# Shared-key attention in a two-layer transformer kernel: two batches as one stream of sixteen units

## The chip, the cores and the metric

The kernel runs on one NeuronCore of a Trainium2 chip. The metric is the device time of one execution in microseconds (us); lower is better. One core has TensorE (PE in the profile, with PEld for its weight loads), VectorE (DVE), ScalarE (ACT), GpSimd (POOL), SyncE (SP) and 16 DMA engines. The engines run their own instruction streams and wait for each other on semaphores.

## What is computed

Two transformer layers run on a residual stream of 2 batches x 2048 tokens x 128 channels. Each layer is an attention followed by a mixture-of-experts feed-forward. The change is in the second of the four parts, the attention inside the first layer's feed-forward block. It has four query heads of 32 channels, but one key and one value of 32 channels that all heads share, and it has no mask. Cut to what matters:

```
nx = rmsnorm(X, g1)
Q = (nx @ Wq.T).reshape(B, S, 4, 32).transpose(0, 2, 1, 3)
Kc = nx @ Wkc.T
Vc = nx @ Wvc.T
scores = jnp.einsum('bhsd,btd->bhst', Q, Kc) * scale
attn = jax.nn.softmax(scores, axis=-1)
out = jnp.einsum('bhst,btd->bhsd', attn, Vc)
```

X is layer-normalized first: the statistics of X are folded into the scale of the rmsnorm (rows `S.mean` and `S.rr` of the code).

## The kernel before

The part is `mqa_attention` (L766). Its work is cut into sixteen **units** of 256 queries x 4 heads; units 0 to 7 belong to the first batch, 8 to 15 to the second. Each unit goes through the 2048 keys of its batch in 16 **tiles** of 128 keys. What happens for a unit U:

- `project`: 12 matmuls make its queries (three products each, of parts split into a high and a low float32r half), and ACT (`q_high`) and DVE (`q_low`) copy them into the buffer `qs`.
- `first_pass`: 32 matmuls of 128 queries x 512 keys, each followed by one max over the 512 keys on DVE (`maxima`, L919). They run through three PSUM banks and only serve to find the maximum of every query; `top`, `max_rows` and `max_row` turn it round into the row that is subtracted. They belong to unit U but run during units U-2 and U-1.
- `scores` (L1182): for each tile two matmuls of 128 keys x 512, into one of two halves of the bank group `stb`; ACT takes the exponential of the tile (L1054, 128x1024) into the ring `pt`.
- `values` (L1193): four matmuls per tile, packed in four column groups, add the values up in `pvb`.
- The softmax's denominators: POOL adds the tiles of `pt` in groups of four, 4, 4, 4 and 2 tiles of a unit (L1095 the first add of a group, L1101 the others: ten adds a unit), and PE sums a group over its keys with `sums` (L1201, four matmuls); the last two tiles go through `last_sums` (L1208) without POOL.
- `close`, `evacuate` (ACT, L1037), `post` (PE L1223, DVE L944 and L946): the result is copied out, turned and divided. This happens at the head of the next unit.

PE's order is written out by hand. It is in order, and so is every other engine. In the main loop a unit is eight pairs of tiles, `gi` 0 to 7: scores of the pair, some first passes, values of the pair before, more first passes. The tables say how many first passes stand in a pair. `EARLY` puts 10 first passes of unit U+2 into pairs 5 to 7 of unit U, after unit U+2 was projected at pair 5 (`TURN`). `LATE` puts the other 22 of unit U+1 into pairs 0 to 4. `ALL` puts all 32 of unit U+1 into pairs 0 to 4, where there were no early ones. In this text pairs 0 to 4 up to ACT's `q_high` are a unit's **head** and the rest is its **tail**; a unit is measured from one `evacuate` to the next.

All of this is done once for each batch. `load(b)` makes the batch's keys and values: DVE normalizes four blocks of 512 tokens (L869), PE turns them (L1112), ACT and DVE split them (L1006, L875), PE projects them (L64 to L66 with `wkv`), the keys go to `ks` (L1017, L886), the values are turned once more (L1121) and go to `v1` (L891). Then the first unit of the batch is projected and its 32 first passes run with nothing beside them but their maxima. `ks` and `v1` exist once, so the second batch can't be loaded before the first has ended. Units 7 and 15 have no first passes to do, units 6 and 14 no early ones. POOL also does small jobs at the start of some units (`between`), and DVE at the end of some: statistics, the splitting of later weights, and in units 11 to 15 the normalized copy `x2` (L968).

Of the kernel before, what the change touches and what calls it, by code (L numbers as in the profile page):

```python
# [759 lines left out]
QUADS_OF_TILES = 3  # L760
ADDS = 3 * QUADS_OF_TILES + 1
SUMS_PER_UNIT = QUADS_OF_TILES + 1
# [3 lines left out]
def mqa_attention(nc, dr, X, g, S, wq, wkv, ao, later, x2):  # L766

    m = Mem(nc, "b1_")
    with m:
# [22 lines left out]
        zeroed = m.sem("zeroed")  # L792
        xn_ready = m.sem("xn_ready")
# [56 lines left out]
        def passes_at(u, g, half):  # L850

            if g >= TURN:
                return (u + 2, EARLY[g][half]) if u + 2 < UNITS else (None, 0)
            if u + 1 >= UNITS:
                return None, 0
            return u + 1, (ALL if u == 0 else LATE)[g][half]

        with nc.Block() as block:
            @block.vector
            def _(dve):  # L860
                def norm(b, i):
# [10 lines left out]
                def x_low(b, i):  # L872
                    dve.wait_ge(xh_ready, b * BB + i + 1)
                    cols = slice(i * BLK, (i + 1) * BLK)
                    nc.vector.tensor_tensor(xl[:, cols], stb[:, i, :], xh[:, cols].bitcast(F32),  # L875
                                            ALU.subtract).then_inc(xl_ready, 1)

                def kv_read(b, i):
# [73 lines left out]
                def between(b, u):  # L952
                    if b == 0 and u in (1, 2):
                        stats_vector(nc, dve, X, S, 1e-6, None, (u + 1,))
                    if b == 0 and u == 3:
                        later.scale(nc, dve, (0, 1, 2))
                    if b == 0 and u == 4:
                        later.scale(nc, dve, (3, 4))
                    if b == 0 and u == 5:
                        later.low(nc, dve, (0, 1))  # L960
                    if b == 0 and u == 6:
# [9 lines left out]
                for b in range(BATCH):  # L971
                    load(b)
                    V = b * UNITS
                    dve.wait_ge(zeroed, 3)
                    q_low(V)
                    maxima(V, 0, P1)
                    top(V)
                    max_row(V)
                    q_low(V + 1)
                    for u in range(UNITS):  # L980
                        U = b * UNITS + u
                        if u > 0:
                            begun = planned(EARLY)
                            if u + 1 < UNITS:
                                maxima(U + 1, begun, begun + LATE[0][0])
                            post(U - 1)
                            begun += LATE[0][0]
                        else:
                            begun = 0
                        if u + 1 < UNITS:  # L990
                            maxima(U + 1, begun, P1)
                            top(U + 1)
                        if u + 2 < UNITS:
                            q_low(U + 2)
                        if u + 1 < UNITS:
                            max_row(U + 1)
# [2484 lines left out]
```

## Time and profile before

| | us |
|---|---|
| median of three runs (2077.88 to 2085.22) | 2085.11 |
| the profiled execution, its own time | 2073.83 |
| its span | 2072.0 |
| first exponential of unit 0 | at 597.63 |
| last evacuation of the first batch (unit 7) | at 841.23 |
| first exponential of unit 8 | at 891.23 |
| last evacuation of the second batch (unit 15) | at 1134.73 |
| PE busy / DVE / ACT / POOL over the span | 1747.5 / 1468.5 / 973.3 / 1032.7 |
| mean granted TensorE clock over the span | 0.924 of full |

Times "at" are from the start of the span of the profiled execution. A busy time is the union of an engine's instructions; a PE matmul's duration includes its pipeline, so that consecutive ones overlap and the distance from start to start is what one costs in a stream. A granted clock of 1.00 is 2.4 GHz, 0.50 is 1.2 GHz; a value between them in a stretch is a mean of the two. Rows in order of time give the start in us, how long it lasted in us, engine, line, operation, output and input, how often it stands there, and in brackets the idle time before it and what ended that. Rows of groups by line give, behind the shapes and the count, the busy us, the mean ns of one, and the idle time before them. "Idle before" is the time in which the engine had nothing to do before an instruction, with what it waited for.

### The profile page before, as it was taken

To read this page: it belongs to the slowest core of one execution; us is meant where nothing else is said; L and a number is where in the kernel's file an instruction comes from. 1 tells how busy PE (TensorE), PEld (TensorE's weight loads), DVE (VectorE), ACT (ScalarE), POOL (GpSimd) and SP (SyncE) were. 2 spreads that over 40 slices of the span, in tenths; PEclk is the share of its full clock that TensorE was granted. 3 is DMA by queue.
4 is the path that set the end of the run, shared out by engine and by line. 5 is a ranking of instruction groups with operands and counts; after the bars stand their busy time and mean duration, and the time that the engine had idled before them with its cause. 6 is when DMAs were issued, how large, how long until landed. Compare 5 with 4: busy or idle time off the path is not lost. (4 is left out here: it accounts for less than half of the span.)

```text
span 2072.0 us, 36812 instructions
## 1 busy us (share of the span) xinstructions
PE 1747.5 (84%) x13548; PEld 1314.7 (63%) x13548; DVE 1468.5 (71%) x3418; ACT 973.3 (47%) x2147; POOL 1032.7 (50%) x685
## 2 busy tenths in 40 slices
PE   3799999998599998799997689947899589978993
PEld 2677787776456664456664567635788467757782
DVE  5688777886588884588884678877777777864234
ACT  2455555565226666246565254423333254325664
POOL 3456555655137898258777156653000310265644
PEclk9899999999679999699999789978999889989997
DMA  5112211221100000000000033329500000016763
GB/s 171 70 70 81 76 66 71 78 80 45 42 1 1 2 1 1 0 1 1 2 1 1 1 103 98 99 79 230 111 1 1 1 1 1 15 51 203 206 219 113
DMA packets 78467, 124.07 MB, mean 60 GB/s; under 512 B 11824, under 2 KB 43440, under 8 KB 77776
## 3 DMA queue, kind: packets, MB, share of 16 engines
q1 hardware_dynamic: 73744, 112.31, 17.9%
q0 software_dynamic: 4544, 9.41, 1.3%
q8 instruction: 108, 1.77, 0.4%
q14 instruction: 71, 0.58, 0.1%
HBM read 59.19 MB, written 28.94 MB: 43 GB/s over the span
## 5 line engine op out<-in xcount | busy, mean ns | idle before, releaser
L1054 ACT ACTIVATE mb_pt<-mb_stb 128x1024 f32<-128x1024 f32 x256 | 249.2, 1020 | 136.5 <-PE mb_stb L1182 127.5
L919 DVE TENSOR_REDUCE mb_mxp<-mb_p1b 128x1 f32<-128x512 f32 x352 | 231.1, 683 | 39.5 <-PE mb_p1b L1166 35.5
L1101 POOL TENSOR_TENSOR mb_psum<-mb_psum,mb_pt 128x1024 f32<-128x1024 f32 x96 | 229.2, 2387 | 19.6 <-ACT mb_pt L1054 7.0
L1095 POOL TENSOR_TENSOR mb_psum<-mb_pt 128x1024 f32<-128x1024 f32 x64 | 152.3, 2380 | 164.0 <-ACT mb_pt L1054 164.0
L351 DVE TENSOR_TENSOR ma_tr<-ma_pbank,ma_cs 128x512 f32<-128x512 f32 x256 | 161.7, 682 | 66.3 <-PE ma_pbank L66 53.6
L2478 PE MATMUL mc_pv<-mc_pt,mc_v 128*128 128x256 f32 x544 | 147.0, 395 | 17.6 <-DVE mc_pt L2281 17.4
L441 POOL TENSOR_TENSOR ma_qt<-ma_tr,ma_swp 128x512 f32<-128x512 f32 x64 | 82.1, 1287 | 158.4 <-DMA ma_swp<-ma_tr 147.4
L1166 PE MATMUL mb_p1b<-mb_ks,mb_qs 96*128 96x512 f32 x352 | 152.7, 479 | 6.6 <-DVE mb_qs L912 3.4
L1182 PE MATMUL mb_stb<-mb_qs,mb_ks 98*128 98x512 f32 x512 | 147.5, 409 | 0.8 <-ACT mb_pt L1054 0.8
L1768 POOL TENSOR_TENSOR mc_frs<-mc_fve,mc_half 128x4 f32<-128x4 f32 x8 | 8.1, 1012 | 272.9 <-DVE mc_fve L1752 272.9
L490 ACT ACTIVATE ma_e<-ma_sbank,ma_mx 128x80 f32<-128x80 f32 x512 | 119.1, 365 | 49.8 <-DVE ma_mx L358 49.8
L1605 POOL TENSOR_TENSOR mb_hh<-mb_hh,mb_gb 128x512 f32<-128x512 f32 x64 | 99.2, 1554 | 83.8 <-DVE mb_hh L1622 55.4
L1193 PE MATMUL mb_pvb<-mb_pt,mb_v 128*32 128x256 f32 x2048 | 138.7, 389 | 0.0
L2281 DVE COPY mc_pt<-mc_tb 128x512 f32<-128x512 f32 (+1 forms) x144 | 94.0, 658 | 60.6 <-PE mc_tb L2463 60.2
L919 DVE TENSOR_REDUCE mb_mxp<-mb_misc 128x1 f32<-128x512 f32 x160 | 109.2, 682 | 15.9 <-PE mb_misc L1166 15.9
L1182 PEld LDWEIGHTS mb_stb<-mb_qs,mb_ks 98*128 98x128 f32 x512 | 95.6, 194 | 36.8 <-issue 9.9
L2478 PEld LDWEIGHTS mc_pv<-mc_pt,mc_v 128*128 128x128 f32 x544 | 95.8, 194 | 35.8 <-DVE mc_pt L2281 26.8
L1166 PEld LDWEIGHTS mb_p1b<-mb_ks,mb_qs 96*128 96x128 f32 x352 | 68.0, 200 | 67.5 <-DVE mb_mxp L919 47.6
L443 POOL TENSOR_TENSOR ma_kt<-ma_tr,ma_swp 128x512 f32<-128x512 f32 x64 | 96.4, 1508 | 27.6 <-DMA ma_swp<-ma_tr 24.7
L3121 POOL DMA_INDIRECT d_ret<-md_ys,md_home x78 | 76.8, 984 | 54.8 <-DVE md_ys L3254 37.8
L500 ACT ACTIVATE ma_pt<-ma_fbank 128x512 f32<-128x512 f32 (+1 forms) x160 | 93.2, 583 | 17.0 <-PE ma_fbank L607 17.0
L64 PE MATMUL ma_pbank<-ma_xth,ma_wh 128*128 128x256 f32 x256 | 84.9, 331 | 15.2 <-DVE ma_tr L351 15.2
(405 smaller groups left out, 4759.2 us busy)
## 6 DMA issues: line engine op xcount, KB each, us to landing
ma_swp<-ma_tr SPq DMA_DIRECT2D x256, 128.0 KB, 2.0
md_wslot<-d_weights SPq DMA_DIRECT2D x39, 516.0 KB, 4.0
d_xs<-mw_blank SPq DMA_DIRECT2D x1, 16899.0 KB, 77.1
mb_gb<-b_gates SPq DMA_DIRECT2D x64, 256.0 KB, 3.3
md_xs<-d_xs SPq DMA_DIRECT2D x39, 131.0 KB, 3.3
md_work<-d_ret SPq DMA_DIRECT2D x8, 512.0 KB, 5.8
mg_X<-x SPq DMA_DIRECT2D x4, 512.0 KB, 9.9
ma_cs<-cs SPq DMA_DIRECT2D x1, 2048.0 KB, 9.8
```

What stands on the lines that cost most here:

```text
L351: nc.vector.tensor_tensor(tr[:, G % TRS, part, :, :], pbank[:, i % 2, :].rearrange("p (c t) -> p c t", c=2), cs[:, b // 2, part, None, :]. ...
L443: nc.gpsimd.tensor_tensor(kt[:, par(b), 2 * c:2 * c + 2, :, PM:KEYS0], t0.rearrange("p c (a b) -> p c a b", b=SEG), t1.rearrange("p c (a b ...
L490: nc.scalar.activation(e[:, s, slot, :], sbank[:, 2 * j + k // 4, k % 4 * KEYS0:(k % 4 + 1) * KEYS0], ACT.Exp, bias=mx[:, s, slot:slot + 1 ...
L919: nc.vector.tensor_reduce(mxp[:, r // NCH, r % NCH:r % NCH + 1], pass_bank(r), AXX, ALU.max).then_inc(p1_max, 1)
L1054: nc.scalar.activation(pt[:, T % RING, :, :].rearrange("p (b h) q -> p b (h q)", b=2), stb[:, 2 * (i % 2):2 * (i % 2) + 2, :], ACT.Exp, sc ...
L1095: nc.gpsimd.tensor_tensor(total, pt[:, T % RING, :, :], pt[:, (T + 1) % RING, :, :], ALU.add).then_inc(summed, 1)
L1101: nc.gpsimd.tensor_tensor(total, total, pt[:, (T + i) % RING, :, :], ALU.add).then_inc(summed, 1)
L1166: nc.tensor.matmul(pass_bank(r), qs[V % 3][0:QROWS, h, t * P:(t + 1) * P], ks[0:QROWS, c * BLK:(c + 1) * BLK], start=True, stop=True).then ...
L1182: last = nc.tensor.matmul(stb[:, 2 * (i % 2) + hp, :], ks[:, i * P:(i + 1) * P], qs[U % 3][:, 2 * hp:2 * hp + 2, :].rearrange("p h q -> p ...
L1193: last = nc.tensor.matmul(pvb[h * DK:(h + 1) * DK, 0:UQ], v1[:, i, :], pt[:, T % RING, h, :], start=(i == 0), stop=(i == KT - 1), skip_gro ...
L1605: nc.gpsimd.tensor_tensor(hh[:, t % HR, :], hh[:, t % HR, :], gb[:, q % GBR, :], ALU.mult).then_inc(gated, 1)
L2478: last = nc.tensor.matmul(pv[:, 0:HC * P], v[:, t, :], pt[:, K % 2, a * HC * P:(a + 1) * HC * P], start=(t == 0), stop=(t == r))
```

## The change

`ks` and `v1` now exist twice, once for each batch, and the main loop runs through sixteen units without a break. `load(0)` stays ahead of it. The second batch's blocks 0 and 1 are loaded inside unit 4 and its blocks 2 and 3 inside unit 5 (`LOADS`), in these steps: ACT normalizes the blocks, after each of tiles 1 to 8, with a bias `nbias` that DVE makes once in unit 3; PE turns both blocks after the values of pair 5, into the banks of `p1b`; ACT copies them before tile 12; PE projects keys and values around the values of pair 6, into `misc` and `p1b`; ACT copies the keys after tiles 13 and 14; PE turns the values in pair 7. DVE's parts stand behind `max_row` in a row. So units 4 and 5 have no early first passes, and units 5 and 6 take `ALL` for the unit after them. Units 6 to 13 have early ones, where units 6 and 7 had none. DVE's two later-weight jobs of units 5 and 6 (`later.low`) move to units 6 and 7. In the last two units POOL adds only pairs of tiles (`TWINS`: seven adds a unit for ten), and PE does seven `sums` for four. GpSimd clears the constant rows of two key buffers instead of one before anything starts, and PE's first instruction waits for both (`zeroed` 4).

```
-QUADS_OF_TILES = 3
-ADDS = 3 * QUADS_OF_TILES + 1
-SUMS_PER_UNIT = QUADS_OF_TILES + 1
+FOURS = [(0, 4), (4, 8), (8, 12), (12, 14)]
+TWINS = [(i, i + 2) for i in range(0, KT - 2, 2)]
+SHORT = 2
+LOADS = {4: (0, 1), 5: (2, 3)}
+SUMMED = [TWINS if U >= 2 * UNITS - SHORT else FOURS for U in range(2 * UNITS)]
...
+        ks = [m.sb(f"ks{b}", [QROWS + 2, SEQ], F32R) for b in range(BATCH)]
+        nbias = m.sb("nbias", [P, BT])
+        v1 = [m.sb(f"v1{b}", [P, KT, DK]) for b in range(BATCH)]
...
+            if g >= TURN:
+                return (u + 2, EARLY[g][half]) if early(u) else (None, 0)
+            if u + 1 >= BATCH * UNITS:
+                return None, 0
+            return u + 1, (LATE if early(u - 1) else ALL)[g][half]
+        def early(u):
+            return 0 <= u and u + 2 < BATCH * UNITS and u not in LOADS
...
             @block.vector
...
+                    if early(U):
+                        maxima(U + 2, 0, planned(EARLY))
+                    for i in LOADS.get(U, ()):
+                        x_low(1, i)
+                    for i in LOADS.get(U, ()):
+                        kv_read(1, i)
+                    for i in LOADS.get(U, ()):
+                        v_read(1, i)
...
             @block.scalar
...
+                        if U in LOADS and 1 <= i <= 2 * BPT:
+                            norm(LOADS[U][(i - 1) // BPT], (i - 1) % BPT)
+                        if i == 2 * TURN and U + 2 < BATCH * UNITS:
+                            q_high(U + 2)
+                        if i == 2 * TURN + 1 and U + 1 < BATCH * UNITS:
+                            max_row(U + 1)
+                        if U in LOADS and i == 2 * TURN + 1:
+                            for k in LOADS[U]:
+                                x_high(1, k)
+                        if U in LOADS and i >= 2 * TURN + 3 and i < 2 * TURN + 5:
+                            k_high(1, LOADS[U][i - 2 * TURN - 3])
...
+                    nc.scalar.activation(xn[:, i % 2, s, :], X[:, BT + tile, :], ACT.Identity, bias=nbias[:, tile:tile + 1],
+                                         scale=S.rr[:, BT + tile:BT + tile + 1]).then_inc(xn_ready, 1)
...
             @block.gpsimd
...
-                nc.gpsimd.memset(ks[QROWS:QROWS + 2, :].bitcast(F32), 1.0).then_inc(zeroed, 1)
-                pool.wait_ge(zeroed, 3)
+                for b in range(BATCH):
+                    nc.gpsimd.memset(ks[b][QROWS:QROWS + 2, :].bitcast(F32), 1.0).then_inc(zeroed, 1)
+                pool.wait_ge(zeroed, 4)
...
             @block.tensor
...
-                for b in range(BATCH):
-                    load(b)
...
+                load(0)
+                project(0)
+                for r in range(P1):
+                    first_pass(0, r)
+                max_rows(0)
+                project(1)
+                for U in range(LAST):
...
+                        if U in LOADS and gi == TURN + 1:
+                            pe.wait_ge(m_row0, 2 * U + 4)
+                            pe.wait_ge(m_row1, 2 * U + 4)
+                            keys_values(1, LOADS[U][0])
+                        if U in LOADS and gi == TURN + 2:
+                            turn_values(1, LOADS[U][0])
...
+                        if U in LOADS and gi == TURN:
+                            pe.wait_ge(q_lo, 2 * U + 6)
+                            for i in LOADS[U]:
+                                turn_in(1, i)
+                        if U in LOADS and gi == TURN + 1:
+                            keys_values(1, LOADS[U][1])
+                        if U in LOADS and gi == TURN + 2:
+                            pe.wait_ge(k_lo, BB + LOADS[U][0] + 1)
+                            turn_values(1, LOADS[U][1])
```

How it moves instructions shows at three places. The first is TensorE's tail of unit 4, from behind the sums of pair 5 into pair 7. L1166 (now L1217) are first passes, L1182 (L1233) scores, L1193 (L1246) values, L1201 (L1254) sums. Before:

```order
L1166 MATMUL mb_p1b<-mb_ks,mb_qs 128x512 x2
L1182 MATMUL mb_stb<-mb_qs,mb_ks 128x512 x4
L1166 MATMUL mb_misc<-mb_ks,mb_qs 128x512
L1166 MATMUL mb_p1b<-mb_ks,mb_qs 128x512
L1193 MATMUL mb_pvb<-mb_pt,mb_v 32x256 x8
L1166 MATMUL mb_p1b<-mb_ks,mb_qs 128x512
L1166 MATMUL mb_misc<-mb_ks,mb_qs 128x512
L1182 MATMUL mb_stb<-mb_qs,mb_ks 128x512 x4
L1166 MATMUL mb_p1b<-mb_ks,mb_qs 128x512 x2
L1193 MATMUL mb_pvb<-mb_pt,mb_v 32x256 x8
L1201 MATMUL mb_pvb<-mb_psum,mb_ones 32x256 x4
L1166 MATMUL mb_misc<-mb_ks,mb_qs 128x512
```

And now:

```order
L1155 MATMUL mb_p1b<-mg_ident,mb_xn 128x128 x8
L1233 MATMUL mb_stb<-mb_qs,mb_ks 128x512 x4
L64 MATMUL mb_misc<-mb_xh,mb_wkv 128x512
L65 MATMUL mb_misc<-mb_xh,mb_wkv 128x512
L66 MATMUL mb_misc<-mb_xl,mb_wkv 128x512
L1246 MATMUL mb_pvb<-mb_pt,mb_v 32x256 x8
L64 MATMUL mb_p1b<-mb_xh,mb_wkv 128x512
L65 MATMUL mb_p1b<-mb_xh,mb_wkv 128x512
L66 MATMUL mb_p1b<-mb_xl,mb_wkv 128x512
L1233 MATMUL mb_stb<-mb_qs,mb_ks 128x512 x4
L1171 MATMUL mb_p1b<-mg_ident,mb_vt 128x32 x4
L1246 MATMUL mb_pvb<-mb_pt,mb_v 32x256 x8
```

The ten first passes of unit 6 are gone (nine of them stand above), and eight turns (L1155), six projections (L64 to L66) and eight turns of values (L1171, the second four behind the next sums) stand in their place.

The second is TensorE at the end of unit 7 and the start of the second batch, before the change; behind these rows stood the other blocks, a projection and 32 first passes alone:

```order
L1201 MATMUL mb_pvb<-mb_psum,mb_ones 32x256 x4
L1193 MATMUL mb_pvb<-mb_pt,mb_v 32x256 x8
L1201 MATMUL mb_pvb<-mb_psum,mb_ones 32x256 x4
L1208 MATMUL mb_pvb<-mb_pt,mb_ones 32x256 x8
L1223 MATMUL mb_pvb<-mg_ident,mb_ots 128x128 x4
L1112 MATMUL mb_stb<-mg_ident,mb_xn 128x128 x12
L64 MATMUL mb_p1b<-mb_xh,mb_wkv 128x512
L65 MATMUL mb_p1b<-mb_xh,mb_wkv 128x512
L66 MATMUL mb_p1b<-mb_xl,mb_wkv 128x512
L1112 MATMUL mb_stb<-mg_ident,mb_xn 128x128 x4
```

In the change these rows are gone from this place: behind the close of unit 7 come the first passes of unit 9 and the scores of unit 8, as in every unit.

The third is GpSimd's last two units. Before, in unit 15, adds in groups of three and a single one at the end:

```order
L1101 TENSOR_TENSOR mb_psum<-mb_psum,mb_pt 128x1024 x2
L1095 TENSOR_TENSOR mb_psum<-mb_pt 128x1024
L1101 TENSOR_TENSOR mb_psum<-mb_psum,mb_pt 128x1024 x2
L1095 TENSOR_TENSOR mb_psum<-mb_pt 128x1024
L1101 TENSOR_TENSOR mb_psum<-mb_psum,mb_pt 128x1024 x2
L1095 TENSOR_TENSOR mb_psum<-mb_pt 128x1024
```

And now, the last rows of the part:

```order
L1138 TENSOR_TENSOR mb_psum<-mb_pt 128x1024
L1143 TENSOR_TENSOR mb_psum<-mb_psum,mb_pt 128x1024 x2
L1138 TENSOR_TENSOR mb_psum<-mb_pt 128x1024
L1143 TENSOR_TENSOR mb_psum<-mb_psum,mb_pt 128x1024 x2
L1138 TENSOR_TENSOR mb_psum<-mb_pt 128x1024 x15
```

The row x15 is the single add of unit 13's last group and the fourteen pair adds of units 14 and 15.

## Rows read from the trace of the kernel before

**Rows 1.** Busy time by stretch (us from the span's start): units, loads, heads
```profile
core 0: us, PE busy (x) PEld busy (x) DVE busy (x) ACT busy (x) POOL busy (x), PEclk, DMA share, GB/s
783.43:812.56 29.13, 26.34 (x237) 14.93 (x238) 16.85 (x30) 17.43 (x20) 25.50 (x11) 1.00 0.00 1
812.56:841.23 28.67, 23.91 (x212) 11.40 (x212) 0.63 (x2) 16.59 (x19) 23.54 (x10) 0.88 0.00 1
841.23:866.00 24.77, 16.07 (x60) 10.64 (x60) 14.95 (x36) 6.53 (x11) 0.00 (x0) 0.60 0.00 1
866.00:891.23 25.23, 23.02 (x49) 12.94 (x50) 21.80 (x39) 1.94 (x5) 0.00 (x0) 0.51 0.00 0
891.23:926.42 35.19, 33.09 (x263) 19.04 (x262) 29.50 (x50) 17.44 (x20) 23.76 (x10) 1.00 0.01 2
926.42:956.53 30.11, 29.77 (x259) 18.32 (x260) 24.23 (x42) 18.05 (x21) 23.75 (x10) 1.00 0.01 1
891.23:914.55 23.32, 21.22 (x134) 12.12 (x133) 20.90 (x36) 10.71 (x11) 17.50 (x8) 1.00 0.00 1
926.42:944.67 18.25, 17.91 (x130) 11.43 (x131) 14.87 (x27) 11.31 (x12) 15.03 (x7) 1.00 0.00 0
1077.03:1105.94 28.91, 26.34 (x237) 14.92 (x238) 24.44 (x38) 16.87 (x19) 23.77 (x10) 1.00 0.00 1
1105.94:1134.73 28.79, 23.94 (x212) 11.42 (x212) 8.68 (x9) 16.02 (x17) 23.66 (x10) 0.88 0.01 2
```

**Rows 2.** ScalarE in order of time: last evacuation, next batch's first exponential
```profile
841.23 0.60 ACT L1037 ACTIVATE mb_ots<-mb_pvb 128x512 f32<-128x512 f32 x1 [3.14 <-PE mb_pvb L1208]
...
891.23 1.94 ACT L1054 ACTIVATE mb_pt<-mb_stb 128x1024 f32<-128x1024 f32 x2
```

**Rows 3.** Groups by line, 540 to 1136 us: GpSimd's adds
```profile
L1101 POOL TENSOR_TENSOR mb_psum<-mb_psum,mb_pt 128x1024 f32<-128x1024 f32 x96 | 229.2, 2387 | 19.6 <-ACT mb_pt L1054 7.0
```

**Rows 4.** All engines in order of time, unit 15
```profile
1110.99 1.94 ACT L1054 ACTIVATE mb_pt<-mb_stb 128x1024 f32<-128x1024 f32 x2 [0.63 <-PE mb_stb L1182]
...
1123.51 1.08 PE L1201 MATMUL mb_pvb<-mb_psum,mb_ones 128*32 128x256 f32 x8 [2.27 <-POOL mb_psum L1101]
...
1125.78 1.94 ACT L1054 ACTIVATE mb_pt<-mb_stb 128x1024 f32<-128x1024 f32 x2 [4.20 <-POOL mb_psum L1095]
...
1129.65 1.94 ACT L1054 ACTIVATE mb_pt<-mb_stb 128x1024 f32<-128x1024 f32 x2 [1.93 <-PE mb_stb L1182]
```

**Rows 5.** TensorE in order of time, unit 10, at the full clock
```profile
957.89 0.60 PE L1223 MATMUL mb_pvb<-mg_ident,mb_ots 128*128 128x128 f32 x4
...
977.60 1.09 PE L1182 MATMUL mb_stb<-mb_qs,mb_ks 98*128 98x512 f32 x4
978.53 0.40 PE L1166 MATMUL mb_misc<-mb_ks,mb_qs 96*128 96x512 f32 x1
...
982.13 1.07 PE L1193 MATMUL mb_pvb<-mb_pt,mb_v 128*32 128x256 f32 x16
...
983.57 0.50 PE L1166 MATMUL mb_misc<-mb_ks,mb_qs 96*128 96x512 f32 x1
```

**Rows 6.** Groups by line, 540 to 1136 us: ScalarE's copies; busy us, mean ns
```profile
L1006 ACT ACTIVATE mb_xh<-mb_stb 128x512 fp32r<-128x512 f32 x8 | 4.8, 597 | 16.1 <-PE mb_stb L1112 16.1
L1949 ACT ACTIVATE mb_wkv<-mb_rkv 128x128 fp32r<-128x128 f32 x1 | 0.3, 292 | 0.0
```

**Rows 7.** VectorE in order of time: units 8, 9 and 10
```profile
892.51 1.29 DVE L919 TENSOR_REDUCE mb_mxp<-mb_p1b 128x1 f32<-128x512 f32 x2 [0.59 <-PE mb_p1b L1166]
...
929.19 0.42 DVE L946 TENSOR_TENSOR mb_ao<-mb_pvb,mb_rd 128x256 f32<-128x256 f32 x1
...
957.86 0.69 DVE L919 TENSOR_REDUCE mb_mxp<-mb_p1b 128x1 f32<-128x512 f32 x1 [1.81 <-PE mb_p1b L1166]
```

**Rows 8.** All engines in order of time, start of the part
```profile
547.99 1.80 POOL L1074 MEMSET mb_ks<- 2x2048 f32 x1
...
549.84 1.97 PE L1112 MATMUL mb_stb<-mg_ident,mb_xn 128*128 128x128 f32 x8 [13.43 <-POOL mb_ks L1074]
```

More of the change, by code:

```diff
@@ L969, in between @@
                                                     ALU.subtract, ALU.mult).then_inc(normed, 1)
-                for b in range(BATCH):
-                    load(b)
[L973 to L996, printed above, removed]
-                        if u + 2 < UNITS:
-                            maxima(U + 2, 0, planned(EARLY))
-                        between(b, u)
-                    post(U)
@@ new lines, in _, with passes @@
+                load(0)
+                project(0)
[3 more added lines that the diff above has]
+                project(1)
+                LAST = BATCH * UNITS
+                done = [0] * LAST
+                for U in range(LAST):
+                    def passes(g, half):
+                        w, count = passes_at(U, g, half)
+                        for _ in range(count):
+                            first_pass(w, done[w])
+                            done[w] += 1
+                    for gi in range(PAIRS_OF_TILES):
+                        if gi == 0 and U > 0:
+                            close(U - 1)
+                        scores(U, 2 * gi)
+                        scores(U, 2 * gi + 1)
+                        if gi == TURN and U + 2 < LAST:
+                            project(U + 2)
+                        if gi == TURN and U + 1 < LAST:
+                            max_rows(U + 1)
+                        if U in LOADS and gi == TURN + 1:
[4 more added lines that the diff above has]
+                            turn_values(1, LOADS[U][0])
+                        passes(gi, 0)
+                        if gi == 0 and U > 0:
+                            post(U - 1)
+                        if gi > 0:
+                            values(U, 2 * gi - 2)
+                            values(U, 2 * gi - 1)
+                        for j, (_, end) in enumerate(SUMMED[U]):
+                            if end // 2 + 1 == gi:
+                                sums(U, j)
+                        if U in LOADS and gi == TURN:
[7 more added lines that the diff above has]
+                            turn_values(1, LOADS[U][1])
+                        passes(gi, 1)
```

238 lines of the change are left out of this document (123 added, 115 removed).

## The prediction

> **What bounds the kernel now.** I read three views in this order: busy time by stretch, each engine in order of time, and groups by line. The busy times show three kinds of stretch [rows 1]. In a unit of the steady stream, such as 926.42 to 956.53, PE is busy 29.8 of 30.11 us at clock 1.00 (units 1 to 5 and 9 to 13 are alike), so PE is the bound. Between the last evacuation of the first batch, 841.23, and the first exponential of the second, 891.23 [rows 2], lie 50.0 us in which ACT works 8.5 us and POOL not at all, at a clock of 0.60 and then 0.51: first the load, a chain handed from engine to engine, then 32 first passes that wait for DVE's maxima. And in units 7 and 15 PE has little to do (23.9 us busy), yet they take 28.67 and 28.79 us: POOL is busy 23.5 to 23.7 of it with ten adds of 2.39 us [rows 3], PE's sums wait 2.27 us for one, and an exponential waits 4.20 us for POOL to leave a slot of the ring [rows 4].
>
> One more price is to be read there. A head with all 32 first passes takes 23.32 us in unit 8, one with 22 takes 18.25 us [rows 1]: 0.51 us for each first pass more, although PE spends only 0.23 us on one (four 512-column matmuls go from 977.60 to 978.53) [rows 5]. The maxima set it: DVE is busy 20.9 of those 23.32 us, and 14.9 of the 18.25 [rows 1]. So heads with ALL are bound by DVE, the rest by PE.
>
> **The change part by part**, against the profiled execution.
>
> 1. The gap between the batches goes. The load, the lone projection and the lone first passes of unit 8 vanish from this place: -50.0 us.
>
> 2. Unit 8 becomes a steady unit, with LATE in place of ALL: 35.19 to 30.11 us [rows 1], -5.1. Unit 7 becomes a steady one: 28.67 to 30.11, +1.4.
>
> 3. Unit 4. Its head stays LATE. In its tail ten first passes go, 10 x 0.23 = -2.3 us of PE. In come 8 turns at 0.15 (four in 0.60) [rows 5], +1.2; six projections of 512 columns at 0.23, +1.4; eight turns of values, taken at the same 0.15, +1.2. Net +1.5 if PE never waits. ACT gets two `x_high` and two `k_high` of 0.60 us each [rows 6] before the last exponentials, 2.4 us, of which steady waits of ACT for scores absorb about one; so the last exponential comes some 1.4 us late, which is the time PE's additions take anyway. DVE loses ten maxima and gets two `x_low`, four copies and subtractions of `kv_read` and two `v_read`, about as much. I take +1.4. The eight norms on ACT are not in the trace; a copy of 128x128 takes 0.29 us [rows 6]. They delay one exponential of each pair by 0.3 us in a head in which ACT idles 6.9 of 18.25 us [rows 1]; bounds 0 and 8 x 0.3 = 2.4; near the lower, 0.2, since scores need them only a pair later. Sum for unit 4: +1.6.
> The Trainium skill (ScalarE: Activation LUTs, What ACT_TABLE_LOAD costs) says that each [128,1] pointer operand adds about 93 ns to an ACTIVATE; these norms have two, the copies of the rows none. By it one norm would take about 0.48 us, an estimate from that page, and the sum would be about 0.3 us higher; no run here shows it yet.
>
> 4. Unit 5 has ALL in its head and the load of blocks 2 and 3 in its tail. The head: the first maximum comes 1.3 us behind the evacuation (957.86 against 956.53); from unit 8's first maximum, 892.51, to the end of its head, 914.55, are 22.0 us; and `post` puts a division of 0.42 us [rows 7] and a smaller reciprocal, together 0.6 by my estimate, between the maxima: 1.3 + 22.0 + 0.6 = 24.0 us [rows 1, 7]. Bounds: 23.3, unit 8's own head, and 25.2, with `post` on PE and some starved maxima added. The tail: 30.1 - 18.25 = 11.9, and +1.4 for the load. So 24.0 + 11.9 + 1.4 = 37.3 for 30.1, +7.2.
>
> 5. Unit 6 has ALL and the full tail: 24.0 + 11.9 = 35.9 for 29.13 [rows 1], +6.8. The second `later.low` jobs that move there stand in DVE's idle end of a tail, as they did: 0.
>
> 6. Unit 15 with pair adds. POOL does 7 x 2.4 = 17 us and no longer holds the ring. A pair of tiles costs PE 0.93 for scores (977.60 to 978.53) and 1.44 for values and sums (982.13 to 983.57) [rows 5], 2.4 together, with issue gaps 2.6. The exponentials of pair 2 begin 5.1 us behind the evacuation (1110.99 against 1105.94), those of pair 7 then five pairs later, and the unit ends 4.4 us behind those (5.1 now, from 1129.65 to 1134.73, less a wait for POOL of 0.7) [rows 1, 4]: 5.1 + 5 x 2.6 + 4.4 = 22.5, from 28.79. Bounds: 21.4 (POOL alone) and 25.4 (PE's present 23.9 busy and three more sums of 0.5). I take 22.4, the pairs at their 2.6 or just under: -6.4. The clock was 0.88 in that unit; with PE busy nearly throughout I expect 1.00.
>
> 7. Unit 14: the same three sums cost 1.5 us and spare about 1.7 us of PE's waits for POOL (its busy PE is 26.3 of 28.91): -0.2.
>
> 8. The start. PE's first turn begins 549.84, when POOL's clearing of 1.80 us ends [rows 8]. A second clearing comes ahead of it: +1.8, with everything behind it, bounds 0 and 1.8; DVE has its first norms ready by then, so nothing covers it.
>
> Sum: -50.0 - 5.1 + 1.4 + 1.6 + 7.2 + 6.8 - 6.4 - 0.2 + 1.8 = **-42.9 us**. The profiled execution took 2073.83, 1.8 more than its span, so it would take 2030.9. Its time is 11.3 below the median of the three runs, 2085.11; the same step from the median gives **2042**.
>
> **The rivals.**
>
> *The load is not hidden.* In units 4 and 5 each step of the load waits for another engine's and PE, in order, stands still meanwhile: turns wait for `q_low`, projections for `x_low`, the last exponential for `k_high`, which waits for a DVE copy. The lone load takes 24.8 us for four blocks with PE busy 16.1 [rows 1]. If half of it, less the projection of unit 8, some 10 us, is added whole to each tail without its first passes (11.9 - 2.3), a tail takes 19.6 for my 13.3, +6.3 twice: -30.3, or 2055. For it: the chain is the same. Against: scores, values and sums now stand between the steps, and the clock is 1.00 there and not 0.60. 11%.
>
> *POOL was not the bound of unit 15*, and three more sums cost what the pair adds give: -36.5, or 2048.6. Against it speak the 4.20 us [rows 4]. 5%.
>
> *Slower: the clock falls in unit 4's tail and stays down.* In the present load it went to 0.60 and stayed at 0.51 through 25 us of first passes in which PE's rows are busy 23.0 us [rows 1]; unit 5's head is of the same kind, bound by DVE. At 1.2 GHz the PE work of units 5 and 6, about 33.5 and 32.1 us (29.8 and the added parts), would take 67 and 64 instead of 37.3 and 35.9, +58, and unit 4's tail, about 10 of PE's work, +10: 68 - 43 = +25, or 2110. It decides where PE's share of work drops as it does in 841 to 866. Against it: unit 8's head is bound by DVE too and shows clock 1.00, with PE busy 21.2 of 23.3 [rows 1]. 2%.
> The Trainium skill speaks for this rival: TensorE: Matmul & The Clock Gate, Part 4: PE-mode transpose, says that transposes do not count as activity for the clock in the way matmuls do, and each loading tail has sixteen. By that rule alone the time would be that rival's; the trace shows the clock low in a load of transposes and waits together, and can't part the two.
>
> *The change does not remove the wait but moves it*: the first pass of unit 8 waits in unit 6 for the last key block, `k_lo`. PE's order has a whole head of 24 us between, so 1%, with the first rival's time.
>
> **How the numbers follow.** The forecast has 81%. What a measurement of this kernel can tell from no change is about 0.5%, 10.4 us. Faster by more: the forecast, the first two rivals and the last, less a little for a sum wrong by over 30 us: 0.96. Slower by more: 0.02. Within: 0.02. The range: the bounds of the heads (-1.4 to +2.4 for two), of the tails (-1 to +5), of unit 15 (-1 to +3) and the start (-1.8) give 2037 to 2053; the runs before spread 7 us downwards from the median, and the first rival reaches 2055. So 2029 to 2057.
>
> **What would show it right or wrong.** Right: no stretch without exponentials between the batches; evacuations 30.1 us apart but for 31.7 (unit 4), 37.3 (5), 35.9 (6), 28.7 (14) and 22.4 (15); the clock 1.00 from unit 0's start to unit 15's end; the last evacuation near 1091.7. The first rival shows as PE idle before L1155, L64 and L1171 in the tails of units 4 and 5, by over 5 us each. The second as unit 15 above 26 us. The clock rival as a granted clock under 0.9 in units 4 to 6. The sum would be wrong as well if the stages behind 1135 us, which the change does not touch, moved by more than 3 us.

## The result and the profile after

The changed kernel takes **2029.95 us** (median of four runs, 2027.06 to 2031.32) against 2081.71 for the kernel before (four runs, 2077.88 to 2085.22): ratio 0.975, 95% interval 0.973 to 0.9771. The forecast was 2042 with a range of 2029 to 2057; the time lies in the range, 1 us above its lower end. The profiled execution took 2031.22 us (span 2029.4) where 2030.9 had been worked out for it.

Busy time by stretch, core 0 of the changed kernel, with the columns of [rows 1]. The first six rows are units 4, 5, 6 and 7 and the heads of units 4 and 5, the next two are units 14 and 15, and the last begins just ahead of unit 0's first exponential and ends with its evacuation:

```profile
725.67:756.68 31.01, 30.45 (x271) 19.05 (x272) 22.67 (x41) 23.88 (x35) 27.04 (x12) 1.00 0.00 1
756.68:793.41 36.73, 34.85 (x281) 20.89 (x282) 27.57 (x49) 23.71 (x35) 25.07 (x11) 1.00 0.00 1
793.41:829.24 35.83, 34.19 (x269) 20.18 (x270) 30.29 (x53) 18.62 (x22) 25.33 (x11) 1.00 0.00 1
829.24:859.36 30.12, 29.79 (x259) 18.34 (x260) 24.23 (x42) 18.64 (x23) 23.75 (x10) 1.00 0.01 2
...
725.67:743.91 18.24, 17.91 (x130) 11.44 (x131) 14.87 (x27) 15.09 (x23) 15.46 (x8) 1.00 0.00 1
756.68:780.61 23.93, 22.27 (x140) 13.25 (x141) 20.72 (x37) 14.93 (x22) 17.58 (x8) 1.00 0.00 1
1039.95:1067.92 27.97, 26.99 (x261) 15.99 (x262) 19.46 (x38) 16.87 (x19) 16.70 (x7) 1.00 0.01 1
1067.92:1089.89 21.97, 21.50 (x236) 11.45 (x236) 10.84 (x9) 16.03 (x18) 16.66 (x7) 1.00 0.01 1
597.00:635.31 38.31, 36.54 (x271) 21.77 (x270) 30.26 (x51) 18.49 (x23) 23.80 (x10) 0.93 0.00 1
```

The 50.0 us between the batches are gone: unit 7 ends at 859.36 and unit 8 lasts 30.1 us like every steady unit. Their price stands in units 4 to 6. Unit 4's head is as before although ACT is busy 15.09 us of it for 11.3 [rows 1]: the eight norms are hidden in ACT's idle time (experiment 5, without them, has the same 18.24). PE is busy through the loading tails, and the clock is 1.00 in them.

PE in order of time, unit 4's tail:

```profile
746.14 1.09 PE L1155 MATMUL mb_p1b<-mg_ident,mb_xn 128*128 128x128 f32 x8
...
746.99 1.18 PE L1233 MATMUL mb_stb<-mb_qs,mb_ks 98*128 98x512 f32 x4
...
748.40 0.47 PE L64 MATMUL mb_misc<-mb_xh,mb_wkv 128*128 128x512 f32 x1 [0.23 <-DVE mb_xl L894]
...
750.27 0.50 PE L64 MATMUL mb_p1b<-mb_xh,mb_wkv 128*128 128x512 f32 x1
...
752.09 0.43 PE L1171 MATMUL mb_p1b<-mg_ident,mb_vt 32*128 32x32 f32 x4
752.46 1.07 PE L1246 MATMUL mb_pvb<-mb_pt,mb_v 128*32 128x256 f32 x16
...
753.89 0.43 PE L1171 MATMUL mb_misc<-mg_ident,mb_vt 32*128 32x32 f32 x4
```

The only wait of PE in the tail is 0.23 us, for `x_low`; unit 5's tail has the same one. Scores and values stand between the steps, as the argument against the first rival had it. Eight turns go in 0.85 us (746.14 to 746.99) and four of values in 0.37 (752.09 to 752.46): 0.11 and 0.09 each where I had taken 0.15. (The 0.15 came from a row's duration of 0.60 us for four, which includes the pipeline; from start to start the same four turns take 0.36, 957.89 to 958.25 in the kernel before.)

At the start (all engines) the second clearing stands in front of PE, as said; with [rows 8] before:

```profile
546.89 4.98 DVE L888 TENSOR_SCALAR mb_xn<-mg_X,mb_mean,mb_rs 128x128 f32<-128x128 f32 x8 [0.93 <-PEq L40]
...
547.27 3.69 POOL L1116 MEMSET mb_ks<- 2x2048 f32 x2
551.01 1.97 PE L1155 MATMUL mb_stb<-mg_ident,mb_xn 128*128 128x128 f32 x8 [15.32 <-POOL mb_ks L1116]
```

And ScalarE in unit 15: a pair takes 2.56 us, and POOL is waited for once, 0.64 us:

```profile
1072.99 1.94 ACT L1088 ACTIVATE mb_pt<-mb_stb 128x1024 f32<-128x1024 f32 x2 [0.64 <-POOL mb_psum L1138]
1075.54 1.94 ACT L1088 ACTIVATE mb_pt<-mb_stb 128x1024 f32<-128x1024 f32 x2 [0.61 <-PE mb_stb L1233]
...
1085.80 1.94 ACT L1088 ACTIVATE mb_pt<-mb_stb 128x1024 f32<-128x1024 f32 x2 [0.63 <-PE mb_stb L1233]
1089.89 0.60 ACT L1073 ACTIVATE mb_ots<-mb_pvb 128x512 f32<-128x512 f32 x1 [2.15 <-PE mb_pvb L1261]
```

### The profile page after: what moved, and what is told of

It reads as the page before. It is cut to its first block and busy times, and to the rows that moved or that the text cites. A ratio compares the mean times of both kernels' runs of the same rounds, so it can differ in the third digit from the quotient of the medians.

```text
span 2029.4 us, 36910 instructions
## 1 busy us (share of the span) xinstructions
PE 1728.3 (85%) x13596; PEld 1311.6 (65%) x13596; DVE 1460.4 (72%) x3403; ACT 979.5 (48%) x2163; POOL 1022.9 (50%) x680
## 5 line engine op out<-in xcount | busy, mean ns | idle before, releaser
L1138 POOL TENSOR_TENSOR mb_psum<-mb_pt 128x1024 f32<-128x1024 f32 x70 | 166.8, 2386 | 131.0 <-ACT mb_pt L1088 130.7
L1143 POOL TENSOR_TENSOR mb_psum<-mb_psum,mb_pt 128x1024 f32<-128x1024 f32 x84 | 200.6, 2388 | 20.0 <-ACT mb_pt L1088 9.8
L2544 PE MATMUL mc_pv<-mc_pt,mc_v 128*128 128x256 f32 x544 | 146.6, 394 | 17.2 <-DVE mc_pt L2347 17.0
L1217 PE MATMUL mb_p1b<-mb_ks,mb_qs 96*128 96x512 f32 x352 | 146.8, 458 | 5.3 <-DVE mb_mxp L938 1.6
L1233 PE MATMUL mb_stb<-mb_qs,mb_ks 98*128 98x512 f32 x512 | 143.1, 401 | 0.4 <-ACT mb_pt L1088 0.4
L1246 PE MATMUL mb_pvb<-mb_pt,mb_v 128*32 128x256 f32 x2048 | 137.3, 386 | 0.0
L1233 PEld LDWEIGHTS mb_stb<-mb_qs,mb_ks 98*128 98x128 f32 x512 | 95.2, 190 | 29.5 <-issue 9.5
L1217 PEld LDWEIGHTS mb_p1b<-mb_ks,mb_qs 96*128 96x128 f32 x352 | 66.1, 195 | 63.1 <-DVE mb_mxp L938 45.2
L64 PE MATMUL ma_pbank<-ma_xth,ma_wh 128*128 128x256 f32 x256 | 85.3, 333 | 16.1 <-DVE ma_tr L351 16.1
```

Source lines behind the costliest of these rows:

```text
L1138: nc.gpsimd.tensor_tensor(total, pt[:, T % RING, :, :], pt[:, (T + 1) % RING, :, :], ALU.add).then_inc(summed, 1)
L1143: nc.gpsimd.tensor_tensor(total, total, pt[:, (T + i) % RING, :, :], ALU.add).then_inc(summed, 1)
L1217: nc.tensor.matmul(pass_bank(r), qs[V % 3][0:QROWS, h, t * P:(t + 1) * P], ks[V // UNITS][0:QROWS, c * BLK:(c + 1) * BLK], start=True, sto ...
L1233: last = nc.tensor.matmul(stb[:, 2 * (i % 2) + hp, :], ks[U // UNITS][:, i * P:(i + 1) * P], qs[U % 3][:, 2 * hp:2 * hp + 2, :].rearrange( ...
L1246: last = nc.tensor.matmul(pvb[h * DK:(h + 1) * DK, 0:UQ], v1[U // UNITS][:, i, :], pt[:, T % RING, h, :], start=(i == 0), stop=(i == KT - ...
L2544: last = nc.tensor.matmul(pv[:, 0:HC * P], v[:, t, :], pt[:, K % 2, a * HC * P:(a + 1) * HC * P], start=(t == 0), stop=(t == r))
```

## The experiments

Unit lengths are read from one evacuation to the next in each profile; units whose work is the same repeat within 0.1 us from run to run, but for the two behind a lone load (unit 0, and unit 8 of the kernel before), while the whole time scatters by several us. So a step of a few us is read from the units, and the median says whether it arrives.

**1. Pair adds undone.**

```
-SHORT = 2
+SHORT = 0
```

> The change with groups of four tiles in units 14 and 15 as well (the pair adds undone alone). If GpSimd's adds set the end of unit 15: unit 14 back from 27.97 to 28.9 us, unit 15 from 21.97 to 28.8, waits for POOL ahead of L1254 and of an exponential, +7.7 us in all. If PE set it and the pair adds only came with something else (the clock of 0.88): under +3 us.

Measured: 2037.51 us (four runs, 2036.53 to 2044.36), +7.6 against the change. Unit 14 is 28.91, unit 15 is 28.81: +0.94 and +6.84. Stretches (the two units), and unit 15 in order of time:

```profile
1042.04:1070.95 28.91, 26.30 (x237) 14.95 (x238) 24.46 (x38) 16.86 (x19) 23.78 (x10) 1.00 0.00 1
1070.95:1099.76 28.81, 21.53 (x212) 10.04 (x212) 8.69 (x9) 16.02 (x17) 23.68 (x10) 1.00 0.01 2
```

```profile
1083.61 4.87 POOL L1143 TENSOR_TENSOR mb_psum<-mb_psum,mb_pt 128x1024 f32<-128x1024 f32 x2
...
1088.53 0.64 PE L1254 MATMUL mb_pvb<-mb_psum,mb_ones 128*32 128x256 f32 x8 [2.29 <-POOL mb_psum L1143]
1089.87 1.94 ACT L1088 ACTIVATE mb_pt<-mb_stb 128x1024 f32<-128x1024 f32 x2 [3.27 <-PE mb_stb L1233]
```

The wait reads as in [rows 4]: PE's sums wait for the last add of a group, and the scores and exponentials behind them wait for PE. The clock was 1.00 here and 0.88 before [rows 1], for the same 28.8 us: the clock was no part of it. The second rival falls.

**2. Pair adds alone, in the kernel before.** Groups and counters as in the change; units 6, 7, 14 and 15 have pairs.

```
+SUMMED = [TWINS if U % UNITS >= UNITS - 2 else FOURS for U in range(2 * UNITS)]
```

> The kernel before with pair adds in units 6, 7, 14 and 15, nothing else changed (one part of the change alone, in both batches). If the adds set it: units 7 and 15 from 28.7 and 28.8 to about 22.0, units 6 and 14 from 29.1 and 28.9 to about 28.0, together -15.4 us, and the 50.0 us between the batches stay. Rival: the last units are short of clock (0.88) and PE work, so three more sums each cost what the adds give, within 3 us of 0.

Measured: 2064.21 us against 2081.39 (ratio 0.9926, 0.9902 to 0.995), -17.2. Units 6, 7, 14 and 15 took 27.95, 21.90, 28.00 and 21.90 us, together -15.8. (The profiled execution took 2065.55 us, only 8.3 less than the first profile: outside the part it took 5.1 us more, and unit 8 2.3 more.) Stretches: unit 7, the gap, unit 8, unit 15:

```profile
815.17:837.07 21.90, 21.43 (x236) 11.44 (x236) 0.63 (x2) 16.59 (x19) 16.58 (x7) 1.00 0.01 1
837.07:887.46 50.39, 39.47 (x109) 24.09 (x110) 36.99 (x75) 8.49 (x16) 0.00 (x0) 0.53 0.00 0
887.46:924.94 37.48, 35.88 (x263) 20.72 (x263) 29.44 (x50) 17.45 (x21) 23.77 (x10) 0.91 0.00 1
1103.46:1125.36 21.90, 21.44 (x236) 11.44 (x236) 10.83 (x9) 16.02 (x17) 16.66 (x7) 1.00 0.01 2
```

The term of unit 15 stands by itself and was worth as much at the end of the first batch. Unasked, unit 8 took 37.48 us at clock 0.91 where it took 35.19 at 1.00 [rows 1]. In both profiles the clock rose within a microsecond of the unit's first exponential; here it fell to 0.50 again 3.3 us later and stayed there for 6.7 us, with the same instructions. In the change, unit 0 did the same on a smaller scale: it took 36.32 us from its first exponential (598.99) to its evacuation, for 35.16, with 3.4 us at 0.50. Stretches: experiment 2's unit 8, then the change's unit 0:

```profile
890.80:897.50 6.70, 6.70 (x28) 4.02 (x27) 4.17 (x8) 1.94 (x2) 5.41 (x3) 0.50 0.00 0
...
602.50:605.90 3.40, 3.40 (x15) 2.07 (x18) 2.58 (x6) 1.94 (x2) 2.47 (x2) 0.50 0.00 0
```

**3. Pair adds in all units.**

```
-SHORT = 2
+SHORT = 2 * UNITS
```

> The change with pair adds in all sixteen units. If PE bounds the steady units: three more sums of 0.5 us each, +1.5 us a unit in the eleven steady ones, less in units 0, 5 and 6, whose heads are VectorE's, +18 to +21 in all. If the adds or the ring bound them instead: 0 or a gain of up to 5 us.

Measured: 2051.97 us, +22.0; steady units take 31.43 us, +1.33, so a sum costs 0.44. PE bounds them. But units 5 and 6 grew as much, by 1.29 and 1.27. The head of a steady unit, and unit 5's head:

```profile
639.26:658.37 19.11, 18.77 (x146) 12.01 (x147) 14.89 (x27) 11.32 (x13) 11.95 (x5) 1.00 0.00 1
803.94:828.74 24.80, 23.14 (x156) 13.82 (x157) 20.72 (x37) 11.89 (x14) 11.87 (x5) 1.00 0.00 1
```

Both heads hold two sums more, and both are 0.87 us longer. So a head with `ALL` isn't bound by DVE alone, as I had put it: with three banks the maxima can't be worked ahead, and when PE does something other than first passes for longer than DVE needs for what lies in the banks, DVE stands still. The rows show it: DVE is busy 20.72 us in unit 5's head with and without the added sums, and two of its waits for a first pass grow from 0.23 to 0.66 us, by one sum each. The first of them, in the change and here:

```profile
768.18 1.29 DVE L938 TENSOR_REDUCE mb_mxp<-mb_p1b 128x1 f32<-128x512 f32 x2 [0.23 <-PE mb_p1b L1217]
...
815.89 1.29 DVE L938 TENSOR_REDUCE mb_mxp<-mb_p1b 128x1 f32<-128x512 f32 x2 [0.66 <-PE mb_p1b L1217]
```

In such a head a first pass costs DVE's time and a sum costs PE's.

**4. The second clearing behind the first load.**

```
+                pool.wait_ge(kv_mm, BB)
+                nc.gpsimd.memset(ks[1][QROWS:QROWS + 2, :].bitcast(F32), 1.0).then_inc(zeroed, 1)
```

> The change with the second key buffer's constant rows cleared only after the first load; PE and DVE wait at the start for the first clearing alone. If nothing covered the second clearing: -1.9 us (the first turn begins 1.9 us earlier, everything behind moves along). Rival: the first norms on DVE would hold the turn anyway, 0.

Start, all engines, with the clearing now at 566.59:

```profile
548.93 3.61 DVE L888 TENSOR_SCALAR mb_xn<-mg_X,mb_mean,mb_rs 128x128 f32<-128x128 f32 x8 [0.93 <-PEq L40]
...
551.17 1.97 PE L1156 MATMUL mb_stb<-mg_ident,mb_xn 128*128 128x128 f32 x8 [13.44 <-POOL mb_ks L1115]
```

The first turn begins 2.24 us behind the first norm, for 4.12 in the change: -1.88, as said. The median, 2030.87 us (2026.31 to 2034.95), doesn't show it; it is smaller than the scatter.

**5. No load for the second batch**, first passes as in the change. The second batch uses the first one's keys, values and tokens. The calls of `norm`, `x_high`, `x_low`, `turn_in`, `keys_values`, `k_high`, `kv_read`, `turn_values` and `v_read` with `LOADS` go, with their waits.

> The change without the second batch's load (no norms, turns, projections or copies in units 4 and 5; the second batch takes the first one's keys, values and tokens), the tables of first passes kept. If PE's additions are the load's price and unit 4 then falls on the adds' pace of 29.1 us that unit 6 had before: unit 4 31.0 to 29.1, unit 5 36.7 to about 33.3 (its tail loses 3.8 us of PE, 0.4 given back to waits), together -5.3 us. If hand-offs between the engines are a large part of it: over -7.6 us, the whole of PE's additions and more.

Measured: 2026.08 us. Units 4 and 5:

```profile
724.87:754.00 29.13, 27.73 (x249) 16.38 (x250) 21.19 (x33) 18.83 (x24) 26.07 (x12) 1.00 0.00 1
754.00:787.36 33.36, 31.69 (x259) 18.38 (x260) 22.95 (x41) 18.62 (x22) 26.25 (x12) 1.00 0.00 1
```

-1.88 and -3.37, together -5.3 us, against 24.8 for the lone load [rows 1]. PE's additions to a tail, as the changed kernel's rows have them, are 0.85 for the turns, 0.74 for those of the values and 1.4 for the projections, 3.0 us; unit 5 gives back 3.4, all of it in its tail (its head is 23.93 us with and without the load), so at most 0.4 is left for hand-offs. Unit 4 gives back only 1.9, since it then falls on GpSimd's pace (busy 26.07 of 29.13). The first rival falls.

**6. The same with the early first passes in every unit.**

```
-LOADS = {4: (0, 1), 5: (2, 3)}
+LOADS = {}
```

> The change without the second batch's load and with the early first passes in every unit (the second batch takes the first one's keys, values and tokens): the full price of hiding the load. If unit 4's tail and the heads with 32 first passes are all of it: units 4, 5 and 6 at 30.1 us each, -13.4 us (0.9 + 6.6 + 5.7 and 0.2 of norms and waits). Rival: something else of the second batch's work delays these units, and less than -10 comes.

Measured: 2016.83 us (2012.16 to 2020.5). Units 4, 5 and 6 at 30.14, 30.14 and 30.12, together -13.2 us against the change. With experiment 5 the price of the hidden load parts in two: 5.3 us for its work, and 7.9 because the ten early first passes of two units had to make room and stand in heads with `ALL`. The load's indirect price is the larger one.

**7. The norms back on DVE, in a block.** ACT's `norm` goes; on DVE behind the division:

```
+                    for i in LOADS.get(U, ()):
+                        norm(1, i)
```

> The change with the second batch's norms on VectorE (16 tensor_scalar behind the division in the heads of units 4 and 5) in place of ScalarE. If unit 4's head is PE's and unit 5's head is VectorE's: unit 4 unchanged (VectorE is busy 14.9 of 18.25 us there; up to +1 if single norms are held up by GpSimd's adds), unit 5 longer by the whole of its eight norms, +2.2 us at 0.28 each and up to +8 at 1.0 each if GpSimd's adds hold them up. Rival: unit 5's head is not VectorE's, 0 for both.

Measured: 2052.42 us, +22. Unit 4 took 43.28 us (+12.3) and unit 5 45.27 (+8.5). I had unit 4 wrong by 11 us. DVE, POOL and PE in order of time, unit 4's head:

```profile
727.17 7.84 DVE L888 TENSOR_SCALAR mb_xn<-mg_X,mb_mean,mb_rs 128x128 f32<-128x128 f32 x8
...
726.72 2.37 POOL L1138 TENSOR_TENSOR mb_psum<-mb_pt 128x1024 f32<-128x1024 f32 x1 [2.21 <-ACT mb_pt L1090]
...
729.23 4.93 POOL L1143 TENSOR_TENSOR mb_psum<-mb_psum,mb_pt 128x1024 f32<-128x1024 f32 x2
...
727.39 0.39 PE L1217 MATMUL mb_misc<-mb_ks,mb_qs 96*128 96x512 f32 x1
735.67 0.80 PE L1217 MATMUL mb_p1b<-mb_ks,mb_qs 96*128 96x512 f32 x1 [7.89 <-DVE mb_mxp L938]
```

And busy time by stretch, from the evacuation to the end of PE's wait, and on:

```profile
724.07:735.60 11.53, 3.72 (x17) 2.63 (x17) 10.17 (x14) 5.25 (x7) 7.60 (x4) 0.84 0.00 0
735.60:745.50 9.90, 9.83 (x45) 5.37 (x46) 5.21 (x10) 1.94 (x2) 2.36 (x1) 0.50 0.00 0
```

Two things add up. Beside GpSimd's adds eight norms take 7.84 us, 0.98 each, where a norm beside nothing takes 0.34, and PE, in order, stands 7.89 us in front of a maximum. The clock falls to 0.50 at about 732, with PE idle since 727.8, and the next 9.9 us of PE's work run at half speed. That is some 4.9 us lost by my estimate (half of 9.9), and with the 7.9 of the wait it is about the 12.3. Unit 5 repeats it with a wait of 6.90 us. So the clock rival's mechanism exists, and here the engine of the norms set it off.

**8. The norms on DVE one by one**, each behind two maxima:

```
+                        for k, (i, s) in enumerate((i, s) for i in LOADS[U] for s in range(BPT)):
+                            maxima(U + 1, begun, begun + 2)
+                            begun += 2
+                            norm_one(i, s)
```

> The change with the norms on VectorE again, but one behind every second maximum in place of eight in a block. If the block alone was the fault (TensorE stood idle 7.9 us behind it and lost its clock): unit 4 within 1 us of 31.0. If VectorE's time is: its 14.9 us of unit 4's head and eight norms of 0.98 make 22.7 for 18.2, so unit 4 at 35 to 36 us and unit 5 at 44 to 45, at clock 1.00.

Measured (one run): 2051.94 us; unit 4 took 38.50, unit 5 took 44.21. Two of the norms in unit 4's head, and the two units:

```profile
736.79 1.39 DVE L895 TENSOR_SCALAR mb_xn<-mg_X,mb_mean,mb_rs 128x128 f32<-128x128 f32 x1
...
741.63 1.75 DVE L895 TENSOR_SCALAR mb_xn<-mg_X,mb_mean,mb_rs 128x128 f32<-128x128 f32 x1
```

```profile
728.01:766.51 38.50, 33.86 (x271) 19.88 (x272) 30.32 (x49) 20.86 (x28) 27.11 (x12) 0.96 0.00 1
766.51:810.72 44.21, 41.39 (x281) 23.45 (x282) 32.96 (x57) 20.67 (x26) 24.96 (x11) 0.85 0.00 1
```

The block was a part (4.8 us of unit 4's 12.3); the other 7.5 stay with the norms one by one. Unit 4 is 2.5 us above what I worked out. Single norms took up to 1.75 us (8.6 for the eight, for 7.8), PE stood in five waits of 0.35 to 1.40 us in front of maxima, and the clock was at 0.50 for 3.5 us. Unit 5's length is as worked out, but not by that working, and that is luck: its eight norms took 6.2 us, and the clock was at 0.50 for 13.6 us in which PE was busy throughout. Unit 5 up to the fall of the clock, and from there to its rise:

```profile
766.51:777.50 10.99, 9.08 (x45) 5.06 (x45) 9.64 (x16) 5.95 (x7) 7.11 (x3) 1.00 0.00 0
777.50:791.10 13.60, 13.54 (x57) 6.71 (x58) 10.38 (x18) 2.96 (x4) 7.07 (x3) 0.50 0.00 1
```

Here no single wait of PE in front of a maximum was longer than 0.67 us before the clock fell. So a long standstill as in experiment 7 isn't needed. How much of unit 5's 7.5 us is the clock and how much DVE's time these rows don't part; half of 13.6 would be an upper estimate for the clock.

**9. A version meant to beat the change**: experiment 4 with groups of three tiles in unit 14; beside it the changed kernel once more, in the same rounds.

```
+THREES = [(0, 3), (3, 6), (6, 9), (9, 12), (12, 14)]
+SUMMED = [FOURS] * (2 * UNITS - 2) + [THREES, TWINS]
```

> A version meant to beat the change: the second clearing behind the first load, and unit 14 with groups of three tiles (five sums and nine adds, for seven and seven; with fours four and ten). If PE's sums now set unit 14 (27.97 us with pairs): two sums fewer at 0.45, 27.1 us, and the start 1.9 us shorter as before, -2.7 us against the change. Rival: nine adds of 2.4 us are late again, unit 14 at 28 to 28.9 as with fours.

> The changed kernel once more, beside the version with the late clearing and the threes, on the same chip and in the same rounds. Units as in its first profile within 0.1 us, but for unit 0, which ends when the clock has risen (36.3 us there, 34.8 to 36.6 in the other variants).

Unit 14 of the version:

```profile
1038.37:1065.74 27.37, 26.39 (x245) 15.33 (x246) 22.70 (x38) 16.86 (x20) 21.46 (x9) 1.00 0.01 1
```

It is 0.6 us shorter than with pairs, where 0.9 was expected; with the start that makes -2.5 in the units. The times are 2030.32 us (six runs, 2025.0 to 2035.97) and 2029.25 (five runs, 2026.01 to 2034.87). So the medians don't show it either, and the version can't be called faster. The changed kernel's units came out as in its first profile, unit 0 at 34.94 us.

**10. The kernel before, twice more.**

> The kernel before, profiled a second time, to see what differs between two of its runs. If the clock's rise behind each of the two lone loads comes at a varying time (the run with pair adds alone took 37.5 us for unit 8 at 0.88 where the first profile had 35.2 at 1.00), then units 0 and 8 here lie between 35.1 and 37.5 us and everything between them is the same within 0.1 us. Rival: the runs differ by the stages around the part alone, units 0 and 8 at 35.2.

> The kernel before, a third profile. Its two profiles so far took 2073.8 and 2075.3 us at a mean clock of 0.924, while its median over the other runs is 2082 and many of those show 0.916 to 0.919. If this run falls among the slower ones, the theory that the clock comes back late behind a lone load puts +2.3 us on unit 8 or unit 0, and the stages around the part hold the rest; units 1 to 6 and 9 to 15 are the same within 0.1 us. Rival: the slower runs are slower everywhere.

Measured: 2075.25 and 2125.03 us. Unit 0 took 35.34 and 35.33 us, 85.06 and 85.07 lie between the evacuations of units 7 and 8 (85.19 in the first profile), the other units are the same within 0.1. Of the third's 50 us more, all stand behind its last evacuation: 990.2 us for 937.3 in the first profile, in stages that the change doesn't touch (the run of the same kernel beside it took 2135.49). The second is as fast as the first and the third differs outside the part, so none of them caught an ordinary slower run. (Unit 8's clock in experiment 2 was 0.91, not 0.88 as the expectation has it.) The profiles of all kernels together do show where executions differ. The stages behind the part, which no edit touches, took 936.2 to 942.9 us in all but the third, and the first turn of the part began between 548.3 and 555.0 us, of which the second clearing explains 1.9; in sum the two make 1487.1 to 1497.5 us. Inside the part the units that an edit leaves alone agree within 0.1 us, but for units 0 and 8.

## Why the prediction was right

Its steps against the two profiled executions:

| step | predicted | measured |
|---|---|---|
| gap between the batches | -50.0 | -50.00 |
| unit 8, unit 7 | -5.1, +1.4 | -5.09, +1.45 |
| unit 4 | +1.6 | +0.89 |
| unit 5 (its head 24.0) | +7.2 | +6.59 (23.93) |
| unit 6 | +6.8 | +6.70 |
| unit 15 | -6.4 | -6.82 |
| unit 14 | -0.2 | -0.94 |
| start (second clearing) | +1.8 | +1.89 |
| unit 0 and the first load | 0 | +1.35 |
| units 1 to 3 and 9 to 13 | 0 | -0.14 |
| stages outside the part | 0 | +1.52 |
| sum | -42.9 | -42.6 |

- **The gap and the steady units** needed no estimate: they are differences of rows, and came out within 0.1.
- **The loading tails** were 0.5 us too dear each: the turns were put at 0.15 us, a duration read as a cost, and took 0.11 and 0.09, 0.8 us less for sixteen. Unit 4's other 0.2 was the term for the norms, which cost nothing. The load took 5.3 us with all it entails (experiment 5), and hand-offs were at most 0.4 of a tail.
- **The norms.** On ACT one takes 485 ns in the mean over sixteen; by the rows of copies I had 0.29. The Trainium skill (ScalarE: Activation LUTs, What ACT_TABLE_LOAD costs) gives 93 ns for each pointer operand, and the estimate from it, 0.48, was right to 0.01 us. It cost nothing either way: unit 4's head is 18.24 us for 18.25, and 18.24 without the norms (experiment 5).
- **The heads with ALL** were right in length (23.93 us for 24.0) and half right in cause: they aren't bound by DVE alone (experiment 3). My 24.0 held because it was taken whole from a head of the same kind.
- **Unit 15** was right in cause and nearly in size (experiments 1 and 2): its three stretches took 5.1, 12.8 and 4.1 us for 5.1, 13.0 and 4.4. In **unit 14** the waits for POOL that pair adds spare were worth more than I gave them: three sums cost 1.3 us and it still gained 0.9, so they spare 2.3 where I had 1.7.
- **The clock.** It stayed at 1.00 in the loading tails with sixteen turns each and in the heads of units 5 and 6, so the rival fell; only unit 0, for which I had 1.00 too, stood at 0.50 for 3.4 us. The Trainium skill's rule that transposes don't count (TensorE: Matmul & The Clock Gate, Part 4: PE-mode transpose) did not decide here, with matmuls between the turns. The rival was closer than its 2%: with the norms on DVE the clock fell in the heads of units 4 and 5, behind a PE that stood still for 7.9 and 6.9 us (experiment 7), and also where no wait of PE before the fall was over 0.67 us (experiment 8, unit 5).
- **The sum** came out 0.3 us off, but in part because its errors cancel: the units and the gap gained 2.6 us more than forecast, and unit 0 and the stages outside the part, both put at 0, lost 2.9.
- **The step that failed** is the last: "the same step from the median gives 2042". From the profiled execution's 2073.83 the sum led to 2030.9, and the changed kernel's median is 2029.95, 12 us under the forecast. Part of it was the three runs: with more of them the median before is 2081.4 (25 runs of the later rounds, 2072.9 to 2086.5). The rest, some 9 us, is that the difference of the medians is -51.8 (-53.4 in the rounds of experiment 9) and that of the profiles -42.6. The bounds of the single steps gave 2037 to 2053; the time lies 7 us below them, and only the 7 us that I had added for the spread of the runs before brought it into the range. That it fell just inside is luck.

What makes this last difference is only partly shown. The clock goes with it: of those 25 runs the ten with a mean granted clock of 0.919 or less took 2083.4 us in the mean, the eleven with 0.923 or more 2078.2, and all nine of the changed kernel had 0.933 to 0.937. Two places where it can arise are shown too. Behind a load that stands alone the clock rises and in some profiles falls back for 3.4 to 6.7 us, which cost unit 8 2.3 us in experiment 2 and unit 0 1.2 in the change. The kernel before has two such loads and the changed one has one. And the stages outside the part scatter by some 10 us in sum (experiment 10); the first profile, from which the forecast started, is among the shortest there, with 1487.1 us; that is 1.5 us less than in the changed kernel's profile, besides the second clearing. But 2.3 and 1.5 us are not 9; no profile caught the kernel before in an ordinary slower run, and the rest stays open.

## What to carry to other kernels

Price a serial stretch that is to be hidden by what must make room for it, not only by its own instructions: here the load's work cost 5.3 us and the displaced first passes 7.9, for 50 won. Before work is moved to an engine with idle time, look at who stands behind it in the queue and at what runs beside it: eight small norms on DVE, with 3.4 us of idle time in the head, cost 12 us because maxima and then PE stood behind them, and PE's clock fell with it. And put a step worked out from one profile on the mean of several profiled runs, or say that the scatter of the runs is the widest term of the range.

## What was unexpected in the hardware

- A DVE norm of 128x128 (`tensor_scalar`, both sides in SBUF) takes 0.34 us alone and up to 2.37 beside GpSimd's adds, as long as one whole add; beside two clearings of 1.84 us each eight of them took 4.98 us, and 3.61 beside one (experiment 4). The maxima, which read PSUM, kept their 0.68 us throughout. The Trainium skill (GPSIMD Engine Reference, 1. Specifications) says that GpSimd shares its SBUF interfaces with VectorE, in contention with DVE instructions that are in a 2-port perf mode or have two SBUF inputs. That the norms are slowed and the maxima are not fits it; in which mode the norms ran no trace shows. The same norms on ACT take 0.48 to 0.49 us, all sixteen, with GpSimd's adds beside them.
- After 7.9 us without work PE was granted 0.50 for the next 9.9 us, in which it was busy nearly throughout; that is some 5 us lost on top of the 7.9, by estimate.
- The clock also fell, for 13.6 us, in a head in which PE was busy 9.08 of the 10.99 us before and never waited longer than 0.67 us for a maximum (experiment 8, unit 5). And behind a lone load it can rise and fall back within the next unit with the same instructions: it didn't in unit 8 of the first profile and did for 6.7 us in experiment 2.
